# A selective-scan kernel on Trainium2: scan tiles of 64 pairs by 16 steps, increments written as pairs of steps, transposes between the first product's blocks

## The chip, the cores and the metric

The program runs on one core of one Trainium2 chip. The metric is the device time of one execution in microseconds (us). A core has TensorE (matmul; the profile shows its weight loads apart, as PEld), VectorE (DVE), ScalarE (ACT), GpSimd (POOL), SyncE (SP, which here only issues DMAs), and 16 DMA engines.

## The reference

Input x is 4 sequences of 2048 tokens with 256 channels. After a layer norm comes a Mamba block (512 inner channels, state 64), then a residual, a second layer norm and a gated FFN:

```
xn = layernorm(x) * ln_w + ln_b
xi, z = split(xn @ W_in)                     # 512 + 512
u = silu(causal_conv4(xi) + conv_b)
dt_r, B, C = split(u @ W_xproj)              # 16, 64, 64
delta = softplus(dt_r @ W_dt + b_dt)
A = -exp(A_log)                              # 512 x 64
for t in range(2048):                        # h: 4 x 512 x 64
    h = h * exp(delta[t] * A) + (delta[t] * u[t]) * B[t]
    y[t] = sum over the state of h * C[t]
block = x0 + ((y + u * D) * silu(z)) @ W_out # x0: the block's input
```

With `block` taken of layernorm(x), the output is:

```
x = x + block(layernorm(x))
x = x + w_down @ (silu(w_gate @ n) * (w_up @ n))   # n = layernorm(x), int weights / 127
```

## The kernel before, in words

Four stages follow each other: `norm_stage`, `project_stage`, `scan_stage`, `output_stage`. Every engine has its own list of instructions, written out by hand in loops; semaphores alone tie them together, so the order on an engine is the order in the code.

**project_stage** makes 16 steps, each over 512 tokens (tile i). TensorE: `front` (16 products `p_in`, L467), `back` (the rows of W_xproj and W_dt, L476 and L482), `turn` (60 transposes of 128x128 bf16 in eight groups, L497). ScalarE copies `xi` (L530), `sz` (L535), `u` (L542), `v`, takes Abs, Exp and Ln, then copies the transposes (`take_turns`, L577, L583). VectorE makes `softplus` (`p_w` L623 is its first row), the convolution of tile i+2 (`front`, L607, L610) and `split`, which divides delta and delta*u into three bf16 parts each (L641 to L647); GpSimd makes delta*u (L681) and the third parts (L685, L687, L689). The transposed parts of delta*u, named `u_turn`, go to the DRAM scratch `u_rows` in eight copies of 512 KB a tile, since one product later multiplies eight combinations of parts of delta*u and B at once. In `step` of TensorE the order is front(i+1), back(i), turn(i), and turn(i) works on the parts of tile i-1.

**scan_stage** makes 256 chunks of 32 steps. A pair is a channel of the lower and one of the upper half: 256 pairs, 64 states each, so that 128 partitions hold both. A chunk has eight tiles of 32 pairs by 32 steps. For a tile, TensorE makes the logits delta*A (L827) into `a_bank`, ScalarE their exponentials (L876) into `decay`; TensorE makes the increments delta*u*B (L849) into `u_bank`; GpSimd multiplies the last column of the chunk before by the first decay (`carry`, L952), adds the chunk's first increment (`seed`, L957) and sets that decay to 0; ScalarE copies `seed` into the first column of `u_bank` (L891); VectorE scans the tile's 1024 elements in one instruction (L917). The product with C (`contract`, L812) goes over the chunk before, two steps of each of four groups at a time, after every second tile. An fp32 product issues twice. `u_bank` holds two tiles: the increments of tile n wait for scan n-2. `H` holds two chunks. SyncE loads a chunk's `x2` (the parts of delta*u) with eight DMAs (L785) once the increments of the chunk before last have been made, and for every second chunk `x1`, `C` and `w2` (the parts of B).

The increment product in the code:

```
dst = u_bank[:, k % 2, 16 * b:16 * b + 16, 8 * e:8 * e + 8]
nc.tensor.matmul(dst.rearrange("p q t -> p t q"), w2[:, g, 4 * s + e, :], x2[:, s, :, e, q:q + 16], ...)
```

`u_bank` has the step innermost and the columns of this product run over the pairs first, so one column lies 32 words of fp32 behind the other.

## Time and profile before

| what | us |
|---|---|
| median of 3 runs (lowest, highest) | 6454.2 (6447.85, 6456.38) |
| the profiled execution's own time | 6459.31 |
| its span in the trace | 6457.5 |
| TensorE busy | 5991.9 (93%) |
| VectorE busy | 5512.5 (85%) |
| ScalarE busy | 3333.9 (52%) |
| GpSimd busy | 2099.4 (33%) |
| DMA moved | 452.03 MB |

How to read it: the shares of busy time are means over four stages. In the trace the transposes of the projection run until 957.85, the scans from 1021.24 to 5775, and the output stage's first DMA is issued at 5786.64; so each stage has to be read by itself. A matmul's end is modelled and matmuls overlap, so TensorE's busy share is not its load.

### The profile page before, as it was taken

The page shows a single profiled execution, that of the slowest core. Times are in us where ns is not written, and L with a number is a line of the kernel's source. Part 1 is how long each engine was busy: PE and PEld are TensorE (multiplying, and loading weights), DVE is VectorE, ACT ScalarE, POOL GpSimd, SP SyncE. Part 2 cuts the span into 40 slices and gives each one's busy share as a digit, 9 for nine tenths or more (in the row PEclk, how much of TensorE's full clock was granted, in tenths as well). Part 3 has the DMA queues.
Part 4 walks back from the last instruction along what each step waited for, and adds up shares of the span by engine and source line. Part 5 has one row for each costly group of instructions (what it writes and reads, how often), then busy time and mean ns, then how long its engine had stood idle before and what let it go on. Part 6 is the DMA issues. An engine that isn't in the chain of part 4 may idle for free. (4 is left out here: it accounts for less than half of the span.)

```text
span 6457.5 us, 156329 instructions
## 1 busy us (share of the span) xinstructions
PE 5991.9 (93%) x46272; PEld 3514.8 (54%) x46304; DVE 5512.5 (85%) x3489; ACT 3333.9 (52%) x7459; POOL 2099.4 (33%) x6848
## 2 busy tenths in 40 slices
PE   2787757999999999999999999999999999988999
PEld 1333324555555555555555555555555555546666
DVE  8566667999999999999999999999999999974443
ACT  1556654555555555555555555555555555541111
POOL 4233334333333333333333333333333333320000
PEclk9887778999999999999999999999999999999999
DMA  4476772111111111111111111111111111123331
GB/s 148 166 239 226 246 258 51 38 37 34 38 36 35 38 36 35 37 36 35 37 36 36 38 35 36 38 35 37 38 34 38 37 34 38 36 58 120 104 104 62
DMA packets 1133185, 452.03 MB, mean 70 GB/s; under 512 B 762608, under 2 KB 1088944, under 8 KB 1132736
## 3 DMA queue, kind: packets, MB, share of 16 engines
q1 hardware_dynamic: 1121456, 438.77, 25.6%
q10 hardware_dynamic: 11664, 12.52, 0.6%
q8 instruction: 26, 0.43, 0.0%
q14 instruction: 39, 0.32, 0.0%
HBM read 229.72 MB, written 221.77 MB: 70 GB/s over the span
## 5 line engine op out<-in xcount | busy, mean ns | idle before, releaser
L917 DVE TENSOR_TENSOR_SCAN s_h<-s_decay,s_ubank 128x1024 f32<-128x1024 f32 x2048 | 4572.2, 2274 | 206.6 <-ACT s_ubank L891 138.0
L876 ACT ACTIVATE s_decay<-s_abank 128x512 f32<-128x512 f32 x4096 | 2223.3, 596 | 1443.3 <-PE s_abank L827 1438.9
L849 PE MATMUL s_ubank<-s_x,s_w 128*128 128x128 bf16 x16384 | 2123.7, 309 | 0.1
L812 PE MATMUL s_ybank<-s_h,s_window 128*16 128x256 f32 x16448 | 1953.7, 603 | 1.8 <-DVE s_h L917 1.8
L849 PEld LDWEIGHTS s_ubank<-s_x,s_w 128*128 128x128 bf16 x16384 | 1715.7, 129 | 73.8 <-DVE s_h L917 0.4
L827 PE MATMUL s_abank<-s_x,s_a 128*128 128x256 bf16 x8192 | 1340.3, 280 | 55.5 <-DMA s_w<-scratch_b_rows 55.5
L952 POOL TENSOR_TENSOR s_carry<-s_decay,s_h 128x32 f32<-128x32 f32 x2016 | 592.2, 294 | 2297.6 <-ACT s_decay L876 2252.4
L827 PEld LDWEIGHTS s_abank<-s_x,s_a 128*128 128x128 bf16 x8192 | 708.2, 108 | 902.9 <-issue 709.0
L812 PEld LDWEIGHTS s_ybank<-s_h,s_window 128*16 128x16 f32 x16448 | 408.5, 104 | 820.0 <-issue 817.3
L957 POOL TENSOR_TENSOR s_seed<-s_carry,s_first 128x32 f32<-128x32 f32 x2048 | 518.2, 253 | 699.6 <-ACT s_first L885 559.2
L959 POOL TENSOR_TENSOR s_decay<-s_none 128x32 f32<-128x32 f32 x2048 | 510.0, 249 | 0.3
L891 ACT ACTIVATE s_ubank<-s_seed 128x32 f32<-128x32 f32 x2048 | 415.2, 203 | 136.8 <-PE s_ubank L849 2.4
L885 ACT ACTIVATE s_first<-s_firstbank 128x256 f32<-128x256 f32 x256 | 98.6, 385 | 450.6 <-PE s_firstbank L838 450.6
L1131 PE MATMUL o_gu<-o_xparts,o_wgu 128*128 128x512 bf16 x1120 | 250.9, 379 | 24.0 <-DVE o_hid L1234 22.2
L1175 ACT ACTIVATE o_sg<-o_gu 128x512 f32<-128x512 f32 x96 | 57.4, 598 | 410.1 <-PE o_gu L1131 409.3
L497 PE MATMUL p_turn<-p_ident,p_uparts 128*128 128x128 bf16 x816 | 96.9, 308 | 159.6 <-POOL p_b_parts L689 74.2
L467 PE MATMUL p_in<-xnT,p_w_in 128*128 (+1 forms) x512 | 228.1, 602 | 15.7 <-DMA p_b_dt<-in_b_dt 12.8
L1131 PEld LDWEIGHTS o_gu<-o_xparts,o_wgu 128*128 128x128 bf16 x1152 | 111.0, 98 | 159.2 <-DVE o_hid L1234 33.0
L497 PEld LDWEIGHTS p_turn<-p_ident,p_uparts 128*128 128x128 bf16 x816 | 79.0, 141 | 197.8 <-issue 119.6
L1141 PE MATMUL o_ob<-o_wd,o_hid 128*128 128x256 f32 x768 | 170.0, 381 | 10.6 <-DVE o_hid L1234 10.6
L467 PEld LDWEIGHTS p_in<-xnT,p_w_in 128*128 128x128 f32 x512 | 97.1, 193 | 136.0 <-issue 111.4
L476 PE MATMUL p_bk<-p_u,p_w_x 128*128 128x512 f32 (+1 forms) x384 | 170.7, 597 | 0.0
(121 smaller groups left out, 3019.2 us busy)
## 6 DMA issues: line engine op xcount, KB each, us to landing
scratch_u_rows<-p_u_turn SPq DMA_DIRECT2D x136, 512.0 KB, 5.7
scratch_delta_rows<-p_dparts SPq DMA_DIRECT2D x128, 512.0 KB, 5.7
s_x<-scratch_delta_rows SPq DMA_DIRECT2D x1024, 64.0 KB, 3.5
s_x<-scratch_u_rows SPq DMA_DIRECT2D x2048, 32.0 KB, 1.7
scratch_y<-s_y SPq DMA_DIRECT2D x1036, 16.0 KB, 1.4
scratch_sz<-p_sz SPq DMA_DIRECT2D x16, 1024.0 KB, 6.7
scratch_u<-p_u SPq DMA_DIRECT2D x16, 1024.0 KB, 8.2
s_w<-scratch_b_rows SPq DMA_DIRECT2D x256, 64.0 KB, 2.4
```

Source lines behind the costliest of these rows:

```text
L467: last = nc.tensor.matmul(in_bank[:, m % 2, :], w_in[:, k, m * P:(m + 1) * P], xnT[:, k, bass.ds(i * TW, TW)], start=(k == 0), stop=(k == ...
L497: last = nc.tensor.transpose(turn_bank[:, g % 2, n * P:(n + 1) * P], src, ident[:, :])
L812: last = nc.tensor.matmul(y_bank[32 * ct:32 * ct + WIN, 0:PAIRS], window[:, s, t * WIN:(t + 1) * WIN], H[s][:, :, t], start=(tt == 0), sto ...
L827: last = nc.tensor.matmul(a_bank[:, b, jj], a_w[:, half, j, :], x1[:, g, :, half, j, s * T:(s + 1) * T], start=True, stop=True)
L849: last = nc.tensor.matmul(dst.rearrange("p q t -> p t q"), w2[:, g, 4 * s + e, :], x2[:, s, :, e, q:q + 16], start=True, stop=True)
L876: nc.scalar.activation(decay[:, k % RING, 16 * b:16 * b + 16, :], a_bank[:, b].rearrange("p j r t -> p (j r) t"), ACT.Exp).then_inc(exp_do ...
L891: nc.scalar.activation(u_bank[:, k % 2, :, 0], seed[:, k % CPS, :], ACT.Identity).then_inc(seeded, 1)
L917: nc.vector.tensor_tensor_scan(H[s][:, PT * k:PT * k + PT, :].rearrange("p q t -> p (q t)"), decay[:, k % RING].rearrange("p q t -> p (q t)"),
L952: nc.gpsimd.tensor_tensor(carry[:, k % CPS, :], decay[:, k % RING, :, 0], before, ALU.mult).then_inc(carried, 1)
L957: nc.gpsimd.tensor_tensor(seed[:, k % CPS, :], carry[:, k % CPS, :], first[:, s, PT * k:PT * k + PT], ALU.add).then_inc(carried, 1)
L959: nc.gpsimd.tensor_tensor(decay[:, k % RING, :, 0], none[:, :], none[:, :], ALU.mult).then_inc(carried, 1)
L1131: last = nc.tensor.matmul(gu[:, m % 2, r, :], wgu[:, r, kk, m * P:(m + 1) * P], xparts[:, part, kk, :], start=(n == 0), stop=(n == 3 * KD ...
```

## The change

In the projection stage the eight groups of transposes are no longer behind `back`; one group stands behind each two products of `front`, on TensorE and on ScalarE, and turn(i) works on the parts of tile i-2. `back` makes the delta products before the rows of B and C, and ScalarE copies `b_in` and `c_out` after Ln. `du_rest` is gone (`du` is overwritten by its rest). `u_turn` becomes fp32: a bf16 part copied into it is the upper half of a word whose lower half is 0. Five copies of 1 MB go to `u_rows` in place of eight of 512 KB. In the diff `...` stands for what is left out.

In the scan stage a tile is 64 pairs by 16 steps (the same 1024 elements); tiles 0 to 3 of a chunk are its first 16 steps, 4 to 7 its last. Even rows r of an 8-step group are read from `u_rows` one bf16 element further on, so that a row of `x2` holds (value, 0) for an even step and (0, value) for an odd one, and one product with 256 columns writes pairs of neighbouring steps. Its loads are sixteen DMAs of 8 partitions. Logits and exponentials run five groups ahead (`LEAD`), `H` holds one chunk, and the first increments are made per half chunk (`firsts`), those of the next chunk's first half at tile 4.

```diff
-PT = 32
-TILES = PAIRS // PT
+TH = T // 2
+PT = 64
+BLOCKS = PAIRS // PT
+TILES = 2 * BLOCKS
+GROUPS = 8
+LEAD = 5
 GP = 2
-COMBOS = [(i, j) for j in range(3) for i in range(3) if i + j < 4]
+PARTS, PLACES = 3, 5
+COMBOS = [(i, j) for i in range(PARTS) for j in range(PARTS) if i + j < 4]
...
-WSTEPS = 8
+COPIES = (2, 2, 1, 1)
+WSTEPS = 4
...
-CONTRACT = {1: (0, 1), 3: (2, 3), 5: (4, 5), 7: (6, 7)}
+CONTRACT = {1: (0, 1), 3: (2, 3)}
...
+        u_turn = sb("p_u_turn", [P, PARTS, SUB, DI])
...
+            def turn_stores(i, last_one=False):
 
                 rows = bass.ds(i * TW, TW)
+                for part in range(3):
+                    sp.wait_ge(turn_read, i * 11 + 13 + 2 * part)
+                    for k, (_, j) in enumerate(COMBOS):
+                        if j == part and k < PLACES:
+                            sp.dma_start(d["u_rows"][rows, k, :].rearrange("(s p) q -> p s q", p=P),
+                                         u_turn[:, j, :, :].bitcast(BF16)).then_inc(turns_stored[j], 16)
...
             def step(i, c, b, ahead1, ahead2):
+                turn_stores(i)
                 if ahead1:
                     front_stores(*ahead1)
-                turn_stores(i)
                 back_stores(i, c, b)
...
             def step(i, c, b, ahead1, ahead2):
-                if ahead1:
-                    front(*ahead1)
+                for m in range(8):
+                    if ahead1:
+                        front(ahead1[0], m)
+                    turn(i, m)
                 back(i, c, b)
...
+                for m in range(8):
+                    if ahead1:
+                        front(ahead1[0], m)
+                    take_turn(i, m)
                 if ahead1:
-                    front(*ahead1)
+                    middle(*ahead1)
                 act.wait_ge(back_ready, i * 7 + 1)
...
+                        (du, du, uparts, (turned, i * 8 + 16), du_done, i + 3, u1_done, ur_done, u2_done)):
...
-                dve.wait_ge(turned, i * 8 + 8)
-                dve.wait_ge(b3_done, i + 1)
+                dve.wait_ge(back_read, i * 7 + 13)
+                dve.wait_ge(turned, i * 8 + 16)
+                dve.wait_ge(b3_done, i + 2)
...
+                pool.wait_ge(u3_done, i + 2)
...
-        H = [sb(f"s_h{s}", [P, PAIRS, T]) for s in range(2)]
-        decay = sb("s_decay", [P, RING, PT, T])
+        H = sb("s_h", [P, 2, PAIRS, TH])
+        decay = sb("s_decay", [P, 3, BLOCKS, PT, TH])
...
+        x2 = sb("s_x2", [P, 2, 4, 4, PAIRS, 2], BF16)
...
+            def widened(r, lo, f):
+
+                src = us[r, 2 * lo:2 * lo + 8, bass.ds(f * 4 + 2 * TW // 8, 4), :]
+                return src if r % 2 else bass.AP(src.tensor, src.offset + 1, src.ap)
...
+                    for lo in range(2):
+                        at = 16 * r + 8 * lo
+                        sp.dma_start(x2[at:at + 8, c % 2, r // 2].rearrange("p e q t -> p e (q t)"),
+                                     widened(r, lo, f)).then_inc(u_loaded[c % 2], 16)
...
+                of, at = (s, 0) if x else (1 - s, TH)
                 for tt in parts:
                     for ct in range(4):
                         t = ct * WSTEPS + tt
...
+            def firsts(it, f, c, x):
+
+                g, s = c // 2, c % 2
+                if x == 0:
+                    pe.wait_ge(u_loaded[s], it * 512 + g * 256 + 256)
+                pe.wait_ge(first_read, f * 2 + x + 1)
+                nc.tensor.matmul(first_bank[:, :, :], w2[:, g, 4 * s + 2 * x, :], x2[:, s, 0, 2 * x],
+                                 start=True, stop=True).then_inc(first_ready, 1)
...
                 s, g = c % 2, c // 2
                 for k in range(TILES):
-                    n = f * TILES + k
+                    n, x, p = f * TILES + k, k // BLOCKS, k % BLOCKS
                     if k == 0:
-                        pe.wait_ge(u_loaded[s], it * 256 + (c // 2) * 128 + 128)
-                        pe.wait_ge(first_read, f + 1)
-                        nc.tensor.matmul(first_bank[:, 0:PAIRS], w2[:, g, 4 * s, :], x2[:, s, 0, 0, :],
-                                         start=True, stop=True).then_inc(first_ready, 1)
-                    if k < TILES - 1:
-                        logits(it, n + 1, c, k + 1)
+                        firsts(it, f, c, 1)
+                    if k == 4 and not last_one:
+                        firsts(it + (c + 1) // 4, f + 1, (c + 1) % 4, 0)
+                    if k + LEAD < GROUPS:
+                        logits(it, f, c, k + LEAD)
                     elif not last_one:
-                        logits(it + (c + 1) // 4, n + 1, (c + 1) % 4, 0)
-                    pe.wait_ge(scan_done, n + 3)
+                        logits(it + (c + 1) // 4, f + 1, (c + 1) % 4, k + LEAD - GROUPS)
+                    pe.wait_ge(scan_done, n + 7)
                     for b in range(2):
-                        q = PT * k + 16 * b
-                        for e in range(4):
-                            dst = u_bank[:, k % 2, 16 * b:16 * b + 16, 8 * e:8 * e + 8]
-                            last = nc.tensor.matmul(dst.rearrange("p q t -> p t q"), w2[:, g, 4 * s + e, :],
-                                                    x2[:, s, :, e, q:q + 16], start=True, stop=True)
+                        q = PT * p + 32 * b
+                        for e in range(2):
+                            dst = u_bank[:, k % 2, 32 * b:32 * b + 32, 8 * e:8 * e + 8]
+                            last = nc.tensor.matmul(dst.rearrange("p q (a t) -> p a q t", t=2), w2[:, g, 4 * s + 2 * x + e, :],
+                                                    x2[:, s, :, 2 * x + e, q:q + 32, :], start=True, stop=True)
                     last.then_inc(u_ready, 1)
-                    if k in CONTRACT:
-                        contract(f, 1 - s, CONTRACT[k])
-
-            logits(0, 0, 0, 0)
+                    if p in CONTRACT:
+                        contract(f, s, x, CONTRACT[p])
...
+            def exps(f, c, kk):
+
+                n, p, at = f * GROUPS + kk, kk // 2, 32 * (kk % 2)
+                step = 1 + c % 2
+                act.wait_ge(scan_done, f * TILES + 1 + p)
                 for b in range(2):
                     act.wait_ge(a_ready, n * 2 + b + 65)
-                    nc.scalar.activation(decay[:, k % RING, 16 * b:16 * b + 16, :],
-                                         a_bank[:, b].rearrange("p j r t -> p (j r) t"),
+                    dst = decay[:, 0:step + 1:step, p, at + 16 * b:at + 16 * b + 16, :]
+                    nc.scalar.activation(dst.rearrange("p x q t -> p q x t"),
+                                         a_bank[:, b].rearrange("p j r (x t) -> p (j r) x t", x=2),
                                          ACT.Exp).then_inc(exp_done, 1)
...
-                    n = f * TILES + k
-                    if k == 0:
-                        dve.wait_ge(y_ready, f + 1)
+                    n, x, p = f * TILES + k, k // BLOCKS, k % BLOCKS
+                    if p == 0:
+                        dve.wait_ge(y_ready, f * 2 + x + 1)
                     dve.wait_ge(carried, n * 3 + 3)
                     dve.wait_ge(seeded, n + 1)
                     nc.vector.tensor_tensor_scan(
-                        H[s][:, PT * k:PT * k + PT, :].rearrange("p q t -> p (q t)"),
-                        decay[:, k % RING].rearrange("p q t -> p (q t)"),
+                        H[:, x, PT * p:PT * p + PT, :].rearrange("p q t -> p (q t)"),
+                        decay[:, x * (1 + c % 2), p].rearrange("p q t -> p (q t)"),
                         u_bank[:, k % 2].rearrange("p q t -> p (q t)"), 0.0,
...
-                    pool.wait_ge(exp_done, n * 2 + 4)
...
+                    n, x, p = f * TILES + k, k // BLOCKS, k % BLOCKS
+                    before = none[:, :] if fresh and x == 0 else H[:, 1 - x, PT * p:PT * p + PT, TH - 1]
+                    decays = decay[:, x * (1 + s), p, :, 0]
+                    pool.wait_ge(exp_done, f * 16 + 4 * p + 6)
...
+    scratch("u_rows", [TOK + 2 * TW, PLACES, 2 * DI], BF16)
```

TensorE's queue in the projection, one step, from its last products on. Before (`p_in` is `front`, `p_bk` is `back`, `p_turn` is `turn`):

```order
L481 REGISTER_ALU
L482 MATMUL p_bk<-p_dtr,p_w_dt 128x512 x2
L481 REGISTER_ALU
L482 MATMUL p_bk<-p_dtr,p_w_dt 128x512
L481 REGISTER_ALU
L482 MATMUL p_bk<-p_dtr,p_w_dt 128x512
L490 ISA
L497 MATMUL p_turn<-p_ident,p_uparts 128x128 x8
L490 REGISTER_ALU
L497 MATMUL p_turn<-p_ident,p_uparts 128x128 x8
L490 REGISTER_ALU
L497 MATMUL p_turn<-p_ident,p_uparts 128x128 x8
```

Now, the end of the first products of a step:

```order
L478 MATMUL p_in<-xnT,p_w_in 128x512 x2
L505 REGISTER_ALU
L512 MATMUL p_turn<-p_ident,p_b_parts 128x128 x8
L476 REGISTER_ALU
L478 MATMUL p_in<-xnT,p_w_in 128x512 x2
L505 REGISTER_ALU
L512 MATMUL p_turn<-p_ident,p_b_parts 128x128 x4
L489 ISA
L490 ISA
L485 MATMUL p_bk<-p_u,p_w_x 16x512 x4
L494 REGISTER_ALU
L495 MATMUL p_bk<-p_dtr,p_w_dt 128x512 x2
```

The transposes have moved from behind the delta products in between the `p_in` products, and the delta products (`p_dtr`) follow the 16-row ones at once.

TensorE's queue in the scan, two tiles and the product with C. Before:

```order
L849 MATMUL s_ubank<-s_x,s_w 128x8x16 x8
L824 ISA
L827 MATMUL s_abank<-s_x,s_a 128x256 x2
L824 REGISTER_ALU
L827 MATMUL s_abank<-s_x,s_a 128x256 x2
L844 REGISTER_ALU
L849 MATMUL s_ubank<-s_x,s_w 128x8x16 x8
L807 ISA
L808 REGISTER_ALU
L812 MATMUL s_ybank<-s_h,s_window 16x256 x8
L824 ISA
L827 MATMUL s_abank<-s_x,s_a 128x256 x2
```

Now, from the increments of tile 3 to those of tile 4:

```order
L891 MATMUL s_ubank<-s_x,s_w 128x4x32x2 x4
L846 MATMUL s_ybank<-s_h,s_window 8x256 x8
L869 ISA
L870 ISA
L871 MATMUL s_firstbank<-s_x,s_w 128x512
L858 ISA
L861 MATMUL s_abank<-s_x,s_a 128x256 x2
L858 REGISTER_ALU
L861 MATMUL s_abank<-s_x,s_a 128x256 x2
L886 REGISTER_ALU
L891 MATMUL s_ubank<-s_x,s_w 128x4x32x2 x4
```

The increments of a tile are four issues in place of eight, and the `first` product of the next chunk (its wait for the loads is L869) stands at tile 4, ahead of that tile's logits and increments.

## Rows read from the trace of the kernel before

**Rows 1.** Page: costliest groups, busy us, mean ns | idle before, releaser

```profile
L917 DVE TENSOR_TENSOR_SCAN s_h<-s_decay,s_ubank 128x1024 f32<-128x1024 f32 x2048 | 4572.2, 2274 | 206.6 <-ACT s_ubank L891 138.0
L876 ACT ACTIVATE s_decay<-s_abank 128x512 f32<-128x512 f32 x4096 | 2223.3, 596 | 1443.3 <-PE s_abank L827 1438.9
```

**Rows 2.** VectorE in order of time, 3008 to 3045: start us, us, what

```profile
3008.19 4.47 DVE L917 TENSOR_TENSOR_SCAN s_h<-s_decay,s_ubank 128x1024 f32<-128x1024 f32 x2 [0.24 <-ACT s_ubank L891]
3012.85 13.67 DVE L917 TENSOR_TENSOR_SCAN s_h<-s_decay,s_ubank 128x1024 f32<-128x1024 f32 x6 [0.19 <-ACT s_ubank L891]
3026.76 4.46 DVE L917 TENSOR_TENSOR_SCAN s_h<-s_decay,s_ubank 128x1024 f32<-128x1024 f32 x2 [0.24 <-ACT s_ubank L891]
```

**Rows 3.** All engines in order of time, 3000 to 3020, same columns

```profile
3003.44 1.04 PE L849 MATMUL s_ubank<-s_x,s_w 128*128 128x128 bf16 x8
...
3009.18 1.90 PE L812 MATMUL s_ybank<-s_h,s_window 128*16 128x256 f32 x16
...
3011.01 0.61 PE L827 MATMUL s_abank<-s_x,s_a 128*128 128x256 bf16 x4
...
3011.46 1.04 PE L849 MATMUL s_ubank<-s_x,s_w 128*128 128x128 bf16 x8
...
3012.61 0.20 ACT L891 ACTIVATE s_ubank<-s_seed 128x32 f32<-128x32 f32 x1
```

**Rows 4.** Matmuls of three lines, ns min/median/max; one in time; windows with PEclk

```profile
L849 PE MATMUL s_ubank<-s_x,s_w x688: 272/314/314, 3002.1 to 3199.2; 128*128 128x128 bf16 x172
...
L827 PE MATMUL s_abank<-s_x,s_a x344: 272/273/314, 3001.6 to 3198.4; 128*128 128x256 bf16 x172
...
L497 PE MATMUL p_turn<-p_ident,p_b_parts x12: 219/219/230, 925.6 to 926.7; 128*128 128x128 bf16 x12
...
924.67 0.62 PE L497 MATMUL p_turn<-p_ident,p_uparts 128*128 128x128 bf16 x8 [0.29 <-ACT p_u_turn L577]
...
3004.00:3041.00 37.00, 37.00 (x324) 21.76 (x322) 35.58 (x17) 21.10 (x53) 12.93 (x53) 1.00 0.18 36
...
923.00:925.00 2.00, 1.16 (x18) 0.82 (x16) 1.97 (x2) 2.00 (x3) 0.00 (x0) 1.00 1.04 354
```

**Rows 5.** SyncE's queue in order of time, 3004 to 3045; last row: us to landing

```profile
3004.69 1.41 SPq L782 DMA_DIRECT2D s_w<-scratch_b_rows  x2
3006.31 4.08 SPq L785 DMA_DIRECT2D s_x<-scratch_u_rows  x8
3010.65 1.91 SPq L767 DMA_DIRECT2D scratch_y<-s_y  x4
...
3029.69 5.92 SPq L777 DMA_DIRECT2D s_x<-scratch_delta_rows  x8
...
s_x<-scratch_u_rows SPq DMA_DIRECT2D x2048, 32.0 KB, 1.7
```

**Rows 6.** All engines in order of time, 500 to 620 (one projection step)

```profile
503.38 1.23 DVE L623 TENSOR_SCALAR p_w<-p_ex 128x2048 f32<-128x2048 f32 x1 [6.59 <-ACT p_ex L566]
...
529.73 0.43 DVE L657 CAST p_b_parts<-p_b_in 128x512 bf16<-128x512 f32 x1
...
544.26 4.18 POOL L687 TENSOR_TENSOR p_uparts<-p_du_rest,p_uparts 128x2048 bf16<-128x2048 f32 x1 [3.49 <-DVE p_uparts L647]
...
548.41 1.15 POOL L689 TENSOR_TENSOR p_b_parts<-p_b_rest,p_b_parts 128x512 bf16<-128x512 f32 x1
...
551.11 1.23 DVE L623 TENSOR_SCALAR p_w<-p_ex 128x2048 f32<-128x2048 f32 x1 [6.59 <-ACT p_ex L566]
...
554.21 1.92 ACT L577 ACTIVATE p_u_turn<-p_turn 128x1024 bf16<-128x1024 bf16 x2
...
555.27 1.95 PE L497 MATMUL p_turn<-p_ident,p_uparts 128*128 128x128 bf16 x16 [3.59 <-ACT p_u_turn L577]
...
561.08 14.23 PE L467 MATMUL p_in<-xnT,p_w_in 128*128 x32
```

**Rows 7.** Stretch of one projection step: busy us per engine, PEclk, DMA share, GB/s

```profile
515.00:563.00 48.00, 37.58 (x126) 17.32 (x125) 32.96 (x29) 29.23 (x38) 17.13 (x6) 0.79 0.69 235
```

More of the change, by code:

```diff
@@ L379, in project_stage @@
         sz_stored = sem("sz_stored")
-        c_stored = [sem("c_stored0"), sem("c_stored1")]
+        c_stored = sem("c_stored")
         dparts_stored = sem("dparts_stored")
-        turns_stored = sem("turns_stored")
+        turns_stored = [sem(f"turns_stored{j}") for j in range(4)]
         n_weights = 10
@@ L452, in _ @@
+            turn_stores(NT + 1, True)
             for s in range(2):
                 sp.wait_ge(u_stored[s], 16 * (NT // 2 + 1))
[L454 removed]
             sp.wait_ge(sz_stored, 16 * (NT + 1))
             sp.wait_ge(dparts_stored, 16 * NCB * (NT + 1))
[L457 removed]
+            sp.wait_ge(c_stored, 16 * (NT + 1))
+            for j in range(4):
+                sp.wait_ge(turns_stored[j], 16 * COPIES[j] * (NT + 3))
@@ L461, in _, with front, rows @@
             pe.wait_ge(weights, 16 * n_weights)
[L463 to L469 removed]
+            def front(i, m):
+                pe.wait_ge(in_read, i * 8 + m + 1)
+                for k in range(KD):
+                    last = nc.tensor.matmul(in_bank[:, m % 2, :], w_in[:, k, m * P:(m + 1) * P],
+                                            xnT[:, k, bass.ds(i * TW, TW)], start=(k == 0), stop=(k == KD - 1))
+                last.then_inc(in_ready, 1)
             def back(i, c, b):
[L472 to L474 removed]
+                def rows(bank, lo, n):
                     for m in range(MI):
@@ new lines, in back, with turn @@
+                rows(0, RANK, 2 * NS)
+                rows(1, RANK + 2 * NS, 2 * NS)
+            def turn(i, g):
+                if g == 0:
+                    pe.wait_ge(u3_done, i + 1)
+                    pe.wait_ge(b3_done, i + 1)
+                pe.wait_ge(turn_read, i * 11 + (9, 11, 12, 13, 14, 15, 16, 17)[g])
+                for n in range(8 if g < 7 else 4):
+                    if g < 6:
+                        at = (2 * (g % 2) + n // 4) * P
+                        src = uparts[:, g // 2, n % 4, at:at + P]
+                    else:
+                        src = b_parts[:, 2 * (g - 6) + n // 4, n % 4 * P:(n % 4 + 1) * P]
+                    last = nc.tensor.transpose(turn_bank[:, g % 2, n * P:(n + 1) * P], src, ident[:, :])
+                last.then_inc(turned, 1)
@@ L816, in contract, with logits @@
                     last.then_inc(y_ready, 1)
-            def logits(it, n, c, k):
-                g, s, half, j0 = c // 2, c % 2, k // 4, 4 * (k % 4)
-                if k == 0 and s == 0:
+            def logits(it, f, c, kk):
+                g, s, half, j0, n = c // 2, c % 2, kk // 4, 4 * (kk % 4), f * GROUPS + kk
+                if kk == 0 and s == 0:
                     pe.wait_ge(rows_loaded[g], it * 176 + 176)
@@ L856, in _ @@
+                    last.then_inc(u_ready, 1)
+                    if p in CONTRACT:
+                        contract(f, s, x, CONTRACT[p])
+            for kk in range(LEAD):
+                logits(0, 0, 0, kk)
+            firsts(0, 0, 0, 0)
             over_chunks_peeled(pe, chunk)
-            contract(NF, 1, tuple(range(WSTEPS)))
+            contract(NF, NF % 2, 0, tuple(range(WSTEPS)))
         @block.scalar
```

256 lines of the change are left out of this document (115 added, 141 removed).

## The prediction

> **What bounds the kernel now.** I read the costliest groups first, then VectorE's rows in order of time, then all engines around one chunk of the scan, then SyncE's queue, then one step of the projection stage, and last the stretches with their clock and DMA share.
>
> The groups [rows 1] say that the time lies in the scan: 2048 scans of 2274 ns are 4657 us of the 6457.5 us span. VectorE's rows [rows 2] show one chunk: 3008.19 to 3026.76 is 18.57 us for eight scans. Six in a row take 13.67 us, so 2.278 us each; eight would take 18.22. What is left is 0.35 us a chunk, in two gaps released by ScalarE's seed copy; over 256 chunks 89 us, the most that the scan stage can give back while its scans stay as they are. (The group's 206.6 us of idle time is too much: 4572.2 / 2.274 is 2011 scans, so 37 of the 2048 are missing from the records and count as idle.)
>
> Why the gap: TensorE [rows 3]. It runs the `y` product from 3009.18 to 3011.08, logits from 3011.01, increments from 3011.46, and ScalarE's seed at 3012.61 follows the increments' end at 3012.50; the scan starts at 3012.85, late. Two tiles of TensorE's work take 4.60 us, VectorE's two scans 4.56: two near-equal bounds. One increment product, 128 columns, takes 314 ns where a transpose of 128 columns at the same granted clock (1.00, so 2.4 GHz) takes 219, and eight come at a spacing of (1.04 - 0.314) / 7 = 0.104 us, as wide as the spacing of logits with 256 columns, (0.61 - 0.273) / 3 = 0.112 [rows 3, 4]. So these write at half the pace of the others; what sets them apart is an output that jumps 128 bytes from column to column.
>
> The projection stage takes 47.7 us a step (503.38 to 551.11) for 16 steps, and no engine is full: in one step TensorE is busy 37.6 of 48, VectorE 33, DMA 0.69 [rows 6, 7]. It is bounded by a chain: the transposes stand behind the last product and before the next step's first one (561.08), and ScalarE copies them between Ln and `xi` (554.21 on).
>
> **The change, part by part.**
>
> *Scan: increments.* 64 products of 128 columns a chunk become 32 of 256, whose inner run is two adjacent steps (8 bytes). Bounds for one: 0.107 us (the pace of the logits) and 0.21 (two of today's). I take 0.107, because the row shows the pace halved for single words and the pair keeps the 8 bytes together. A tile's increments then take 0.43 us instead of 0.86, two tiles save 0.86, and TensorE's 4.60 falls to about 3.75, well under 4.56. VectorE's gap goes: -89 us.
>
> *Scan: the rest of the tile.* The scan stays 128x1024, and products of `y` stay at 16 issues every second tile. Exponentials keep their 512 elements, now in runs of 16, and I take today's 596 ns [rows 1]; nothing in the rows has such runs. Walking one pair from the end of a scan at 0: increments 0.1 to 0.7, `y` product to 2.3, logits' first half at 2.7, two exponentials to 3.9, seed to 4.2; the scan it feeds is due at 4.56. So 0.3 us cover a dearer exponential; beyond that each excess costs four times a chunk. GpSimd's three operations a tile grow from 32 to 64 elements; it is busy 12.93 of 37.00 us [rows 4], and twice that still fits. `take_y` and `firsts` come twice a chunk: 0.8 us of ScalarE more in 18.2, behind the seed; hidden.
>
> *Scan: loads of the increments' operand.* This is where a wait is added. Eight loads a chunk become sixteen on SyncE's queue, and the first product that needs them moves from tile 0 to tile 4 of the chunk before. Today eight loads take 4.08 us from 3006.31, 0.51 each, and land 1.7 us after issue [rows 5]; in even chunks two loads of `w2` come first, so they begin 1.83 us after the increments that free the buffer ended (3004.48) [rows 3, 5]. Bounds for a new one: 0.48 (a store of `y`, 16 packets, 1.91 us for four) and 0.74 (a load of `x1`, 512 packets, 5.92 us for eight). It has 32 packets of 1 KB instead of 64 of 512 B, so I take 0.51. The last lands at 1.83 + 15 x 0.51 + 1.7 = 11.2 after the buffer is free, which is 11.9 after the scan end that I count from. TensorE reaches tile 4 at four scans (9.1) + 0.1 + 0.4 + 1.8 = 11.4. Behind it wait logits, increments, exponentials and the seed: 11.9 + 0.1 + 0.2 + 0.4 + 1.1 + 0.4 = 14.1; the scan is due at six scans, 13.67. So even chunks lose 0.45 us, odd ones (no `w2`, 1.6 earlier) nothing: 128 x 0.45 = +58 us. SyncE's issue time for two chunks is about 1.4 + 2 x 4.1 + 2 x 1.9 + 5.9 = 19.3 us and rises to 27.5 of 36.4, so it is no bound by itself.
>
> *Scan: ends.* The first chunk waits for eight more loads: +4. The last `y` product is half as long (32 issues of 0.107 less): -3.
>
> *Projection.* Transposes of tile i-2 now stand between the products of tile i+1, ScalarE takes them between `xi` and `sz`, and the delta products come before those of B and C. The old chain breaks up. What is late next: the single copy of `uparts`. From the first transposes to the last are 7 products of 14.23 / 8 = 1.78 us and 7.5 groups of eight at half of (1.95 - 0.25), 0.85: 18.8 us. Then VectorE splits, 529.73 to 544.26, 14.5 us; GpSimd takes the last parts, 4.2 + 1.15; hand-overs 0.5. Sum 39.2 us, and I take 39.3 [rows 6]. Bounds: 36.2 us from the DMAs, and 47.7 (nothing gained). For the DMAs: 235 GB/s at a share of 0.69 is 341 at full; a step moves 11.3 MB and five stores of 1 MB instead of eight of 0.5 add 1.05: 12.3 / 0.341 = 36.2 [rows 7]. Fifteen intervals, the last without a product: 14 x 8.4 + 2 = -120 us. The second extra round of transposes is in the old tail already, since the last tile's were waited for there too: 0.
>
> **Sum.** -120 - 89 + 58 + 4 - 3 = -150. The profiled execution took 6459.3 us, so 6309; the median of the runs shown is 5 us lower, so **6304**.
>
> **A rule against the trace.** The half pace of the scattered writes is this trace's own [rows 4]. The Trainium skill, "PSUM — Partial Sum Buffer", section "Specifications (TRN2)", gives 8-byte cachelines and adds that any non-contiguous pattern slows matmuls significantly. The first half fits pairs at full pace; the second half, read strictly, leaves them slow, which is the first rival.
>
> **Rivals.**
> 1. *Pairs write no faster per column.* For it: the output still jumps 64 bytes after every pair. Against: nothing in the rows has pairs. TensorE keeps 4.60 us for two tiles and gets two `first` products of 512 columns where it had one of 256, at the logits' 0.112 per 256 columns 0.34 us more: 18.57 + 0.34 = 18.91 a chunk, +87 us. With -120 and +1: **6422**. By the strict reading of that page this would be the outcome.
> 2. *Everything in time.* The sixteen loads land before tile 4, and TensorE, with fewer pauses, keeps the upper clock in the transposes (a group of eight took 0.62 us at clock 1.00, against half of 1.95 [rows 4, 6]), so that the step falls to the DMAs' 36.5: 14 x 11.2 + 2 = -159, -89, +1: **6207**.
> 3. *The loads decide (slower).* Place: the wait for `u_loaded` before `firsts` at tile 4. If a load takes 0.65 us instead of 0.51 (half-way to `x1`'s), even chunks lose 0.45 + 15 x 0.14 = 2.55 us and odd ones 0.93, 3.48 a pair: 128 x 3.48 - 89 = +356, and with -120 **6691**. It turns the sign from 1.6 us a pair, a load of 0.59. For it: the new loads reach 8 partitions, and half of them start 2 bytes off. Against: issue time hardly depends on packets (0.48 with 16, 0.51 with 64).
> 4. *The projection gains little*, because stores of 0.94 DMA share hold back buffers or VectorE and GpSimd slow each other: 45 us a step, -40, -31: **6383**.
>
> **Chances.** The forecast 0.55, rival 1 0.13, rival 2 0.15, rival 3 0.10, rival 4 0.07. A measurement of this kernel tells 0.2% (13 us) from no change. Rival 3 is slower by more than that, with 0.01 for others: 0.11; 0.04 within it (the upper end of rival 1, a mild form of 3); 0.85 faster. The range runs from rival 2 to the upper side of rival 1, 6205 to 6440, and leaves out rival 3 and half of rival 2's lower side.
>
> **What would show it.** Increments of 256 columns at a median near 273 ns and a group of four in about 0.6 us (rival 1: 480 and 0.9); scans back to back, a chunk of 18.2 us odd and 18.7 even, the gap in front of tile 4 with a DMA as TensorE's releaser; the interval between two `p_w` on VectorE at 39 us, with VectorE waiting for transposes before the cast of `b_parts`; DMA share there above 0.9; the output stage unchanged. I am wrong if the scans themselves lengthen, if the gaps move to another tile with ScalarE's exponentials as releaser, or if the step stays over 43 us.

## The result and the profile after

| what | before, us | after, us |
|---|---|---|
| median (lowest, highest), 4 runs each | 6455.29 (6447.85, 6457.26) | 6155.88 (6154.45, 6157.07) |
| span of the profiled execution | 6457.5 | 6152.6 |
| up to the first scan | 1021.2 | 928.4 |
| first scan to the end of the last | 4753.8 | 4547.5 |
| behind the last scan | 682.5 | 676.7 |

The ratio is 0.954, 95% interval 0.952 to 0.956. The forecast of 6304 us had the sign, and 148 us too little gain; its range ended at 6205. Of 304.9 us of span, 92.8 were gained up to the first scan, 206.3 in the scan stage (forecast: 31) and 5.8 behind it.

The page of the changed kernel, costliest groups (busy us, mean ns | idle before, releaser):

```profile
L971 DVE TENSOR_TENSOR_SCAN s_h<-s_decay,s_ubank 128x1024 f32<-128x1024 f32 x2048 | 4499.2, 2267 | 81.6 <-ACT s_ubank L940 80.4
L923 ACT ACTIVATE s_decay<-s_abank 128x512 f32<-128x512 f32 x4096 | 2234.9, 604 | 1763.5 <-PE s_abank L861 1763.5
...
L861 PE MATMUL s_abank<-s_x,s_a 128*128 128x256 bf16 x8192 | 1425.4, 276 | 310.9 <-DMA s_x<-scratch_u_rows 73.6
```

A scan's record is hardly shorter than before (2267 ns against 2274, [rows 1]), and the exponentials in their runs of 16 take 604 ns against 596. VectorE in order of time (start us, us, what, [idle before <- releaser]):

```profile
2989.65 26.37 DVE L971 TENSOR_TENSOR_SCAN s_h<-s_decay,s_ubank 128x1024 f32<-128x1024 f32 x12
3016.34 35.15 DVE L971 TENSOR_TENSOR_SCAN s_h<-s_decay,s_ubank 128x1024 f32<-128x1024 f32 x16 [0.32 <-ACT s_ubank L940]
3051.92 35.15 DVE L971 TENSOR_TENSOR_SCAN s_h<-s_decay,s_ubank 128x1024 f32<-128x1024 f32 x16 [0.42 <-ACT s_ubank L940]
```

Sixteen scans take 35.15 us, 2.197 each, where [rows 2] gave 2.278: less than the 2.26 us that a record lasts, so neighbouring records overlap. Two chunks take 3051.92 - 3016.34 = 35.58 us against 2 x 18.57. One gap is left in two chunks; TensorE's queue in order of time shows what it waits for, and SyncE's what came late:

```profile
3011.73 0.61 PE L891 MATMUL s_ubank<-s_x,s_w 128*128 128x256 bf16 x4
3012.27 1.90 PE L846 MATMUL s_ybank<-s_h,s_window 128*8 128x256 f32 x16
3014.68 0.60 PE L861 MATMUL s_abank<-s_x,s_a 128*128 128x256 bf16 x4 [0.52 <-DMA s_x<-scratch_u_rows]
```

```profile
3003.79 1.43 SPq L813 DMA_DIRECT2D s_w<-scratch_b_rows  x2
3005.52 7.24 SPq L818 DMA_DIRECT2D s_x<-scratch_u_rows  x16
3013.03 1.71 SPq L799 DMA_DIRECT2D scratch_y<-s_y  x4
```

Four increment products of 256 columns take 0.61 us where eight of 128 took 1.04 [rows 3]: pairs write at full pace, as forecast. TensorE's wait stands at tile 4 with a DMA behind it, as forecast, and VectorE's gap is 0.32 to 0.42 us against 0.45. The sixteen loads take 7.24 us, 0.45 each (0.51 taken).

One projection step, VectorE, GpSimd and the last transposes of TensorE in order of time:

```profile
496.85 4.18 POOL L713 TENSOR_TENSOR p_uparts<-p_du,p_uparts 128x2048 bf16<-128x2048 f32 x1 [3.49 <-DVE p_uparts L672]
497.02 5.09 DVE L650 TENSOR_SCALAR p_w<-p_ex 128x2048 f32<-128x2048 f32 x1
500.99 2.13 POOL L715 TENSOR_TENSOR p_b_parts<-p_b_rest,p_b_parts 128x512 bf16<-128x512 f32 x1
502.14 3.13 DVE L652 SCALAR_TENSOR_TENSOR p_ex<-p_w,p_ex 128x2048 f32<-128x2048 f32 x1
...
509.84 5.94 DVE L634 TENSOR_SCALAR p_acc<-p_xi,p_conv_w 128x512 f32<-128x512 f32 x4
510.06 4.63 POOL L707 TENSOR_TENSOR p_du<-p_lw,p_u 128x2048 f32<-128x2048 f32 x1 [6.94 <-DVE p_lw L658]
...
520.59 0.39 PE L512 MATMUL p_turn<-p_ident,p_b_parts 128*128 128x128 bf16 x4
...
524.02 0.43 DVE L682 CAST p_b_parts<-p_b_in 128x512 bf16<-128x512 f32 x1
...
530.08 4.99 POOL L711 TENSOR_TENSOR p_dparts<-p_w,p_dparts 128x2048 bf16<-128x2048 f32 x1 [3.49 <-DVE p_dparts L672]
531.17 6.04 DVE L670 TENSOR_TENSOR p_du<-p_du,p_uparts 128x2048 f32<-128x2048 f32 x1
538.73 5.08 DVE L650 TENSOR_SCALAR p_w<-p_ex 128x2048 f32<-128x2048 f32 x1
```

The step is 538.73 - 497.02 = 41.7 us, against 47.7 before and 39.3 forecast. The addition `p_w` took 1.23 us [rows 6] and takes 5.09 beside GpSimd's 4.18: it ends 1.1 us after GpSimd has ended. Two signs that the forecast named are absent: VectorE doesn't wait for transposes ahead of the cast of `b_parts` (the last of them ended 3.0 us earlier), and the DMA share is 0.83 and not above 0.9. A window over five steps (busy us of PE, PEld, DVE, ACT, POOL; PEclk, DMA share, GB/s) has VectorE busy nearly all the time, 198 of 200 us:

```profile
450.00:650.00 200.00, 178.40 (x609) 77.98 (x608) 198.18 (x142) 138.59 (x175) 84.73 (x25) 0.87 0.83 294
```

### The profile page after: what moved, and what is told of

The parts are those of the page before. It is cut to its first block and busy times, and to the rows that moved or that the text cites. A ratio compares the mean times of both kernels' runs of the same rounds, so it can differ in the third digit from the quotient of the medians.

```text
span 6152.6 us, 147986 instructions
## 1 busy us (share of the span) xinstructions
PE 5492.5 (89%) x37915; PEld 2419.3 (39%) x38396; DVE 5559.3 (90%) x3491; ACT 3328.5 (54%) x7982; POOL 2612.2 (42%) x6848
## 5 line engine op out<-in xcount | busy, mean ns | idle before, releaser
L971 DVE TENSOR_TENSOR_SCAN s_h<-s_decay,s_ubank 128x1024 f32<-128x1024 f32 x2048 | 4499.2, 2267 | 81.6 <-ACT s_ubank L940 80.4
L846 PE MATMUL s_ybank<-s_h,s_window 128*8 128x256 f32 x16416 | 1948.2, 602 | 1.9 <-DVE s_h L971 1.9
L1008 POOL TENSOR_TENSOR s_carry<-s_decay,s_h 128x64 f32<-128x64 f32 x2032 | 882.3, 434 | 1781.3 <-ACT s_decay L923 1030.3
L891 PE MATMUL s_ubank<-s_x,s_w 128*128 128x256 bf16 x8192 | 1234.7, 273 | 38.3 <-DVE s_h L971 4.0
L891 PEld LDWEIGHTS s_ubank<-s_x,s_w 128*128 128x128 bf16 x8192 | 735.9, 98 | 288.3 <-DVE s_h L971 183.0
L1012 POOL TENSOR_TENSOR s_seed<-s_carry,s_first 128x64 f32<-128x64 f32 x2048 | 657.9, 321 | 164.4 <-ACT s_first L929 4.0
L846 PEld LDWEIGHTS s_ybank<-s_h,s_window 128*8 128x8 f32 x16416 | 377.2, 97 | 838.6 <-issue 835.5
L1014 POOL TENSOR_TENSOR s_decay<-s_none 128x64 f32<-128x64 f32 x2048 | 619.9, 303 | 0.0
L940 ACT ACTIVATE s_ubank<-s_seed 128x64 f32<-128x64 f32 x2048 | 495.8, 242 | 72.6 <-PE s_ubank L891 9.1
L996 POOL TENSOR_TENSOR s_window<-s_c,s_none 64x32 f32<-64x32 f32 x512 | 130.7, 255 | 406.8 <-PE s_ybank L846 386.6
L913 ACT ACTIVATE s_y<-s_ybank 128x256 f32<-128x256 f32 x514 | 198.4, 386 | 6.8 <-PE s_ybank L846 6.8
```

The costliest lines, as they stand in the source:

```text
L846: last = nc.tensor.matmul(y_bank[32 * ct:32 * ct + WIN, 1 - x, :], window[:, of, (at + t) * WIN:(at + t + 1) * WIN], H[:, 1 - x, :, t], st ...
L891: last = nc.tensor.matmul(dst.rearrange("p q (a t) -> p a q t", t=2), w2[:, g, 4 * s + 2 * x + e, :], x2[:, s, :, 2 * x + e, q:q + 32, :], ...
L940: nc.scalar.activation(u_bank[:, k % 2, :, 0], seed[:, k % CPS, :], ACT.Identity).then_inc(seeded, 1)
L971: nc.vector.tensor_tensor_scan(H[:, x, PT * p:PT * p + PT, :].rearrange("p q t -> p (q t)"), decay[:, x * (1 + c % 2), p].rearrange("p q t ...
L1008: nc.gpsimd.tensor_tensor(carry[:, k % CPS, :], decays, before, ALU.mult).then_inc(carried, 1)
L1012: nc.gpsimd.tensor_tensor(seed[:, k % CPS, :], carry[:, k % CPS, :], first[:, x, PT * p:PT * p + PT], ALU.add).then_inc(carried, 1)
```

## The experiments

Two questions: why the scan stage gained 206 us where 89 was held to be the most, and why the step stopped at 41.7 us.

**1. The kernel before, increments written flat.**

```diff
-dst = u_bank[:, k % 2, 16 * b:16 * b + 16, 8 * e:8 * e + 8]
+bank = u_bank[:, k % 2, 16 * b:16 * b + 16, :].rearrange("p q t -> p (q t)")
+dst = bank[:, 128 * e:128 * e + 128].rearrange("p (t q) -> p t q", q=16)
...
```

> The kernel before, its increments written as 128 consecutive words a product instead of words 128 bytes apart. The words land in other places of the bank, so the kernel computes other states; amount and kind of work are those of before. Theory (TensorE set the scan stage, its scattered increments with it, and VectorE's own spacing is the 2.197 us of the changed kernel): increments 314 -> about 220 ns, a group of eight about 0.6 us instead of 1.04, scans at 2.197 us, a chunk 17.6 us instead of 18.57, time 6455 - 256 x 0.97 = about 6207. Rival (2.278 us is the scan's own pace in the layout of 32 pairs by 32 steps, and the changed kernel is faster by its layout of 64 by 16): a chunk 18.22 us, time 6455 - 89 = about 6366. Rival (the pace of a product doesn't depend on where it writes): 314 ns and 6455 unchanged.

Measured: 6164.3 us, ratio 0.955 (0.953 to 0.957), with nothing else of the change in it. Increments take 219 ns. Those products (ns min/median/max):

```profile
L850 PE MATMUL s_ubank<-s_x,s_w x736: 218/219/231, 3000.9 to 3198.8; 128*128 128x128 bf16 x184
```

VectorE in order of time:

```profile
2997.90 52.36 DVE L918 TENSOR_TENSOR_SCAN s_h<-s_decay,s_ubank 128x1024 f32<-128x1024 f32 x24
```

24 scans of the old layout at 52.36 / 24 = 2.18 us. The layout of the changed kernel is not the cause; TensorE was, through its scattered writes. [rows 4] had it: TensorE was busy 37.00 of 37.00 us there, VectorE 35.58. The flat kernel gave 43 us more than my 6207, since even 2.197 was not the floor.

**2. The changed kernel, single words again.**

```diff
-matmul(dst.rearrange("p q (a t) -> p a q t", t=2), ..., x2[:, s, :, 2 * x + e, q:q + 32, :])
+matmul(dst.rearrange("p q (a t) -> p a t q", t=2), ..., x2[...].rearrange("p a q t -> p a t q"))
```

> The changed kernel, with the order in which an increment product writes turned round: the steps of a pair are no longer written one behind the other, so that each word lands 64 bytes from the one before. Same values in the same places. Theory (pairs are what made the products quick, and TensorE becomes the bound again without them): a product of 256 columns about 0.21 us instead of 0.107 in a row, two tiles of TensorE 4.6 us or more, a chunk 18.6 to 18.9 us instead of 17.8 on average, time 6156 + 256 x 1.0 = 6360 to 6450. Rival (the scans are quicker for another reason than TensorE, their new layout): scans stay at 2.197 us, time within 20 us of 6156.

Measured: 6422.4 us, 267 more than with pairs. The increment products (ns min/median/max, and four of them in order of time):

```profile
L891 PE MATMUL s_ubank<-s_x,s_w x342: 379/417/418, 3001.0 to 3200.0; 128*128 128x256 bf16 x171
...
3010.51 1.03 PE L891 MATMUL s_ubank<-s_x,s_w 128*128 128x256 bf16 x4
```

VectorE in order of time:

```profile
3007.33 9.05 DVE L971 TENSOR_TENSOR_SCAN s_h<-s_decay,s_ubank 128x1024 f32<-128x1024 f32 x4 [0.43 <-ACT s_ubank L940]
3016.72 9.05 DVE L971 TENSOR_TENSOR_SCAN s_h<-s_decay,s_ubank 128x1024 f32<-128x1024 f32 x4 [0.34 <-ACT s_ubank L940]
```

417 ns instead of 273, four in 1.03 us instead of 0.61, and four scans at 9.05 us, 2.26 each, without a shown gap: the slow spacing of [rows 2] comes back with TensorE's load. A chunk is 2 x 9.39 = 18.8 us. Experiments 1 and 2 settle it from both sides.

With that known, [rows 2] can be read again. Single scans of the kernel before (ns min/median/max, start of the first and the last):

```profile
L917 DVE TENSOR_TENSOR_SCAN s_h<-s_decay,s_ubank x2: 2262/2274/2287, 3010.4 to 3012.8; 128x1024 f32<-128x1024 f32 x2
...
L917 DVE TENSOR_TENSOR_SCAN s_h<-s_decay,s_ubank x2: 2262/2274/2287, 3012.8 to 3015.0; 128x1024 f32<-128x1024 f32 x2
...
L917 DVE TENSOR_TENSOR_SCAN s_h<-s_decay,s_ubank x2: 2262/2274/2287, 3015.0 to 3017.4; 128x1024 f32<-128x1024 f32 x2
```

The starts are 2.4, 2.2, 2.4 us apart. In the row "x6, 13.67 us" every second scan was late by about 0.2 us: 0.08 of it is hidden in the overlap of the records, and the rest was too short to break the row. A late scan reads 2287 ns, a prompt one 2262. Two scans are 4.6 us apart (3010.4 to 3015.0, 3012.8 to 3017.4), which is TensorE's 4.60 for two tiles.

**3. First products behind tile 6 instead of tile 4** (`if k == 4` becomes `if k == 6`, on TensorE and ScalarE).

> The changed kernel, with the first products of the next chunk's first half put behind tile 6 instead of tile 4. Theory (they wait there for the loads of delta*u in even chunks, and that wait is the 0.42 us gap of VectorE): the gap goes, a chunk is 8 x 2.197 = 17.58 us in both kinds, time 6156 - 128 x 0.42 = about 6102, and TensorE shows no wait for a DMA. Rival (the 0.9 us of first products, now a tile closer to the increments that need them, makes another scan late): the gap moves to tile 7 or 0 of the next chunk and the time is 6156 or above.

Measured: 6090.8 us, 65 less, the whole of it between first and last scan (4547.5 to 4482.6). TensorE's list of waits has no DMA left, and VectorE runs without a break:

```profile
2999.01 52.60 DVE L971 TENSOR_TENSOR_SCAN s_h<-s_decay,s_ubank 128x1024 f32<-128x1024 f32 x24
```

So the late loads cost 65 / 128 = 0.51 us per even chunk. The gap of 0.42 us showed this too small, by the 0.08 us that two records overlap otherwise.

**4. GpSimd's third part of delta*u nearly left out.**

```diff
-nc.gpsimd.tensor_tensor(uparts[:, 2], du[:, :, :], uparts[:, 1], ALU.subtract)
+nc.gpsimd.tensor_tensor(uparts[:, 2, :, 0:16], du[:, :, 0:16], uparts[:, 1, :, 0:16], ALU.subtract)
```

> The changed kernel; of the third bf16 part of delta*u GpSimd makes only 16 of 512 columns, the rest stays zero, so GpSimd's 4.17 us beside VectorE's p_w addition are nearly gone. Theory (GpSimd's operation holds VectorE's up, and VectorE is the bound of the projection step): p_w takes 1.23 us as alone, instead of 5.09, the step falls from 41.7 to 37.9 us, time 6156 - 15 x 3.8 = about 6099. Rival (p_w is slow because of the DMA traffic or its operands): p_w stays at 5.09 and the time near 6156. Rival (VectorE isn't the bound): p_w 1.23, VectorE waits instead, step and time unchanged.

Measured: 6099.7 us and a step of 37.95, as the theory had it:

```profile
512.13 1.33 DVE L650 TENSOR_SCALAR p_w<-p_ex 128x2048 f32<-128x2048 f32 x1
...
550.08 1.33 DVE L650 TENSOR_SCALAR p_w<-p_ex 128x2048 f32<-128x2048 f32 x1
```

GpSimd's operation causes the 5.09 us, and VectorE is the bound: what it no longer loses, the step gains in full.

**5. `p_w` on ScalarE** (activation Identity with a bias of 1.0, in place of VectorE's addition).

> The changed kernel, with the addition p_w = ex + 1 made by ScalarE (1.9 us, behind its exponential) instead of VectorE. Theory (VectorE bounds the step of 41.70 us; what GpSimd's 4.17 us of work holds up is whichever VectorE operation stands beside it, so the subtraction that now stands there is held up in place of p_w): only the addition's own 1.23 us go, step about 40.5, time 6156 - 15 x 1.2 = about 6138. Rival (only the cheap one-operand additions are held up): all 5.09 us go from VectorE and the chain of my forecast takes over at 39.2 us, time 6156 - 15 x 2.5 = about 6118, with VectorE idle. Rival (VectorE isn't the bound): 6156 or, if ScalarE's 1.9 us stand in the chain, up to 6185.

Measured: 6141.0 us, 15 less, as the theory had it (6138). The hold-up has passed to the operation behind (2.29 us when alone):

```profile
532.22 4.19 POOL L717 TENSOR_TENSOR p_uparts<-p_du,p_uparts 128x2048 bf16<-128x2048 f32 x1 [3.49 <-DVE p_uparts L676]
...
532.89 5.67 DVE L656 SCALAR_TENSOR_TENSOR p_ex<-p_w,p_ex 128x2048 f32<-128x2048 f32 x1 [0.41 <-ACT p_w L587]
```

**6. Transposes behind all first products again.**

```diff
                 for m in range(8):
                     if ahead1:
                         front(ahead1[0], m)
+                for m in range(8):
                     turn(i, m)
```

(ScalarE's copies likewise.)

> The changed kernel, with the eight groups of transposes and their copies all behind the eight first products again, and everything else left (sizes, VectorE's and GpSimd's order, delta products first). Theory (VectorE is the bound at 41.7 us, interleaving hides work that was hidden by then): step within 1 us of 41.70, time 6150 to 6170. Rival (the interleaving is what brought the step down from 47.7): step 45 to 48 us, time 6156 + 15 x 3.3 to 6.3 = 6205 to 6250, VectorE idle before p_w with ScalarE's exponential as releaser.

**7. The products of B and C first again**, with ScalarE's copies of them; interleaving kept.

> The changed kernel with the products of B and C ahead of the delta products again (and ScalarE's copies with them); interleaved transposes stay. Theory (VectorE bounds the step; this order gives slack that isn't used): 41.7 us as before, 6150 to 6165, maybe a wait of 1 us at p_w. Rival (the early delta products are what brought 47.7 down): they come about 8 x 0.7 = 5.7 us later, step 44 to 47.7, time 6190 to 6245.

**8. Both moves undone.**

> The changed kernel with both moves undone: transposes behind all first products and products of B and C first. What is left of the change in this stage is that tile i-2 is transposed instead of i-1, the same for the stores, and the double time that the split parts may stay. Theory (each move alone gives enough slack, both together are needed to undo it): p_w waits again for ScalarE's exponential, step 44 to 47.7, time 6190 to 6245. Rival (the lag of two tiles alone is what took the transposes out of the chain): 42 to 43 us, time 6155 to 6180.

Measured: 6166.3 us (6), 6160.9 (7), 6259.9 (8). Either move alone brings nearly all, since 10 and 5 us are what its absence costs; without both, 104 are lost, the step is 47.7 us on average (772.63 - 247.84 over 11), and the old wait is back, in VectorE's row of the last kernel:

```profile
514.50 1.23 DVE L652 TENSOR_SCALAR p_w<-p_ex 128x2048 f32<-128x2048 f32 x1 [9.88 <-ACT p_ex L589]
```

What (8) leaves of the change in this stage (the lag of two tiles, the fp32 `u_turn`, the five copies of 1 MB) gives nothing by itself.

The expectation for (7), that VectorE bounds the step and has slack, held for the time and not for the mechanism. VectorE's row there:

```profile
548.02 1.42 DVE L650 TENSOR_SCALAR p_w<-p_ex 128x2048 f32<-128x2048 f32 x1 [3.59 <-ACT p_ex L587]
```

VectorE waits 3.6 us for ScalarE, GpSimd's 4.18 us pass meanwhile, and `p_w` takes 1.42 us instead of 5.09: the wait stands where the hold-up stood, and the step stays at 41.7. That the early delta products would be worth more in a kernel without the hold-up follows from this row; no run shows it.

**9. Three edits: experiments 3 and 5, and the first tap of the convolution on ScalarE.**

> The changed kernel with three edits together: first products behind tile 6, p_w on ScalarE, and the first tap of the convolution (four products with a constant, 5.94 us a step beside GpSimd) on ScalarE too. Scan stage as with the first edit alone: -65. Projection, theory (VectorE is the bound, GpSimd's two long operations of 4.17 and 4.63 us then hold up the operations behind): of 41.70 go 1.23 and four times 0.35 us, 41.70 - 2.6 = 39.1, time 6156 - 65 - 15 x 2.6 = about 6052. Rival (the operations that come beside GpSimd now are not held up): 5.1 + 5.9 us go and the chain of my forecast binds at 39.2 or ScalarE's work (30.5 + 4.3 us busy, with its table loads) does: 6050 to 6060 as well, but with VectorE idle 8 us a step and its operations at the length that they have alone. Rival (ScalarE becomes the bound): step above 41.7, time above 6091.

Measured: 6059.2 us, with a step of 39.35 us on average. The time lies near the theory's 6052 and within the first rival's 6050 to 6060, so the rows have to tell them apart. GpSimd, TensorE and VectorE in order of time:

```profile
523.12 4.20 POOL L721 TENSOR_TENSOR p_uparts<-p_du,p_uparts 128x2048 bf16<-128x2048 f32 x1 [3.49 <-DVE p_uparts L680]
527.28 3.20 POOL L723 TENSOR_TENSOR p_b_parts<-p_b_rest,p_b_parts 128x512 bf16<-128x512 f32 x1
530.72 0.62 PE L515 MATMUL p_turn<-p_ident,p_uparts 128*128 128x128 bf16 x8 [1.94 <-POOL p_b_parts L723]
...
534.87 12.30 DVE L648 SCALAR_TENSOR_TENSOR p_acc<-p_xi,p_conv_w,p_acc 128x512 f32<-128x512 f32 x12
...
535.10 4.90 POOL L715 TENSOR_TENSOR p_du<-p_lw,p_u 128x2048 f32<-128x2048 f32 x1 [4.62 <-DVE p_lw L666]
...
547.94 0.39 PE L515 MATMUL p_turn<-p_ident,p_b_parts 128*128 128x128 bf16 x4
548.37 0.43 DVE L690 CAST p_b_parts<-p_b_in 128x512 bf16<-128x512 f32 x1 [0.99 <-PE p_turn L515]
```

The twelve taps take 12.30 us where the changed kernel has 8.03: held up again, by 4.3, which speaks against that rival. But VectorE is no longer the bound either (busy 185 of 200 us). In every second step it waits for the transposes ahead of the cast of `b_parts`, which starts 0.04 us after the last of them has ended: the chain of the forecast binds there, with 39.8 us from cast to cast (508.60 to 548.37). It was a true bound, but not the first one. Its total came out by two errors that nearly cancel: the split takes 14.5 us as forecast, GpSimd's last parts 7.4 where 5.35 were taken (`p_b_parts` takes 3.20, not 1.15), and the transposes 17.6 where 18.8 were taken.

**10. All five GpSimd operations of the step on VectorE**, on top of experiment 3.

```diff
+dve.wait_ge(two, i + 1)
+nc.vector.tensor_tensor(parts[:, 2], rest[:, :, :], parts[:, 1], ALU.subtract).then_inc(three, 1)
...
+nc.vector.tensor_tensor(du[:, :, :], lw[:, :, :], u[:, c % 2], ALU.mult).then_inc(du_done, 1)
```

> The changed kernel with first products behind tile 6 (6091 us), and GpSimd's five operations of the projection step put on VectorE, each at the place where its result is due. Theory (beside each of GpSimd's operations VectorE stands still for nearly all its time, so GpSimd gives nothing and costs its slower pace): of VectorE's 41.7 us about 12.4 are held-up time (3.9 at p_w, 0.8 at p_ex, 4.0 at the first tap, 2.9 and 0.8 at the two subtractions); they go, and three operations of 2.3 and two of 0.6 us come: 41.7 - 12.4 + 8.1 = 37.4 us a step, time 6091 - 15 x 4.3 = about 6026. Rival (the two engines do overlap, the rows only share the delay out otherwise): VectorE gets 8.1 to 18 us more to do, a step of 45 or more, time above 6140.

**11. The same with experiment 9's two edits.**

> As the kernel before in this list, with p_w and the first tap on ScalarE as well. Theory: VectorE falls to 37.4 - 1.2 - 2.0 = 34.2 us and something else takes over: the DMAs (share 0.88 at a step of 39.8 us in the kernel with three edits, so 35 us at full) or ScalarE (34.3 us busy); a step of 35 to 36.5 us, VectorE with 1 to 3 us idle, time 6091 - 15 x 5.5 = about 6005 to 6015. Rival (VectorE still sets it, by the handovers to ScalarE in the softplus): 37 us or more, time 6020 or above.

Measured: 6018.2 us (10) and 6017.1 (11). VectorE's step in (10), in order of time:

```profile
502.36 2.29 DVE L674 TENSOR_TENSOR p_uparts<-p_du,p_uparts 128x2048 bf16<-128x2048 f32 x1
...
505.63 1.22 DVE L650 TENSOR_SCALAR p_w<-p_ex 128x2048 f32<-128x2048 f32 x1
...
542.30 1.22 DVE L650 TENSOR_SCALAR p_w<-p_ex 128x2048 f32<-128x2048 f32 x1
```

The window over five steps of it:

```profile
450.00:650.00 200.00, 189.47 (x651) 80.96 (x650) 195.53 (x184) 155.25 (x195) 0.00 (x0) 0.92 0.95 337
```

A step of 542.30 - 505.63 = 36.7 us with GpSimd idle (the theory had 37.4 us and 6026). VectorE needs 2.29 us for what took GpSimd 4.18 and cost VectorE 3.9 meanwhile. The held-up time, from 41.70 to 36.67 with 8.25 us of work added, is 13.3 of GpSimd's 18.0 us a step. In (11) VectorE is unloaded by 2.9 us more and nothing comes of it; its window shows what is full now, TensorE (190 of 200) and the DMAs (0.95):

```profile
450.00:650.00 200.00, 189.94 (x659) 81.15 (x658) 179.97 (x158) 177.45 (x226) 0.00 (x0) 0.92 0.95 335
```

The list of waits of this window names no DMA. TensorE's own pauses end with ScalarE: at `p_sz` 5.1 us in five waits, at `p_dtr` 4.1 in six. So the trace points to TensorE and its hand-overs with ScalarE and not to the DMAs; no run takes load off TensorE alone, so it isn't shown by an edit. The expectation for (11), 6005 to 6015 us from a step of 35 to 36.5, failed: unloading VectorE gained 1 us, which is no difference between these runs.

**12. First products at tiles 5 and 1 instead of 6 and 0**, on top of experiment 10.

> The kernel with GpSimd's projection work on VectorE (6018 us, first products at tiles 6 and 0), with the first products moved to tiles 5 and 1. At even tiles they stand behind the product with C, on TensorE's longest stretch, and the kernel before with flat increments runs its scans at 2.179 us, this one at 2.189; one scan in four or so is 2289 ns long instead of 2261. Theory (the scan behind such a first product is released late by 0.05 to 0.1 us, and no idle time shows): scans at 2.18 us, all near 2261 ns, 2048 x 0.010 = -20 us, time about 5998. Rival (GpSimd's wider operations hold the scans up, or the scan's pace depends on the layout): 6018 unchanged.

Measured: **5993.3 us**, ratio to the kernel before 0.9285 (0.927 to 0.930), the best of all. VectorE in order of time:

```profile
2999.34 61.06 DVE L966 TENSOR_TENSOR_SCAN s_h<-s_decay,s_ubank 128x1024 f32<-128x1024 f32 x28
```

All its scans in 200 us (ns min/median/max):

```profile
L966 DVE TENSOR_TENSOR_SCAN s_h<-s_decay,s_ubank x93: 2261/2261/2262, 2999.3 to 3199.7; 128x1024 f32<-128x1024 f32 x93
```

None of these 93 scans reads 2287 ns any more. The scan stage takes 4461.2 us, 2.178 a scan, the same as experiment 1's 4461.7 in the other layout: this is the pace of such scans when their operands lie ready, and the least that any run here needed.

## Why the prediction was wrong

*Increments.* Right: pairs at the pace of the logits, 0.107 us in a row taken, 0.60 to 0.61 us for four measured. Rival 1 is out, and so is the strict reading of the Trainium skill, "PSUM — Partial Sum Buffer", section "Specifications (TRN2)": a pattern that jumps 64 bytes after every 8 was not slowed. With single words (experiment 2) it was, to half the pace: four in 1.03 us.

*VectorE's gap, -89: the step that failed.* "Six in a row take 13.67 us, so 2.278 us each; eight would take 18.22. What is left is 0.35 us a chunk ... the most that the scan stage can give back." The division took six scans that TensorE released late for six at VectorE's own pace. The two bounds named as near-equal, 4.60 and 4.56 us for two tiles, were one: the second was the first seen through VectorE. VectorE's own was 2 x 2.178 = 4.36, so a chunk could shrink from 18.57 us to 17.42. With the loads in time (experiment 3) it came to 4482.6 / 256 = 17.51: 4753.8 to 4482.6, -271 instead of -89. The trace of the kernel before held the warning, and the forecast argued it away. It took 37 scans to be missing from the records, since 4572.2 us of busy time are only 2011 times 2.274. None is missing: all 2048 are there, and neighbouring records overlap by 0.08 us. So 4753.8 - 4572.2 = 181.6 us of idle time in the scan stage were real, twice the 89.

*Loads late, +58.* Right in place, kind and chunk; +65 measured by experiment 3. Rival 3 is out. The size is partly luck: the sixteen loads were issued in 7.24 us and not in 8.2, which makes the wait shorter, and the scans that TensorE follows came at 2.2 us and not at 2.278, which makes it longer.

*Start and ends, +4 and -3.* The output side came to -5.8. The start isn't seen apart from the projection.

*Projection, -120.* -93 up to the first scan. The chain of 39.2 us is real (experiment 9), but VectorE was costed by its busy time in the kernel before, 33 of 48 us, and the new order puts `p_w`, the operation behind it and the first taps beside GpSimd, which adds 3.9 + 0.8 + 4.0 us: 41.7. The kernel before had shown such a hold-up, in a subtraction that takes 2.29 us when GpSimd is idle (experiment 10):

```profile
535.79 4.98 POOL L685 TENSOR_TENSOR p_dparts<-p_w,p_dparts 128x2048 bf16<-128x2048 f32 x1 [3.49 <-DVE p_dparts L647]
536.88 6.04 DVE L645 TENSOR_TENSOR p_du_rest<-p_du,p_uparts 128x2048 f32<-128x2048 f32 x1
```

The forecast had this as half of rival 4, at 45 us and a chance of 0.07. The Trainium skill has the mechanism in "SBUF — State Buffer", section "SBUF: two separate sides": VectorE and GpSimd share a pair of ports under an exclusive lock, held for a whole instruction, and it concerns VectorE where it reads two inputs from SBUF or runs in a two-port mode. The trace agrees (5.09 us beside 4.18, 1.23 alone), and the scans, which read one input from PSUM, were not held (2261/2261/2262 ns with GpSimd at work). Whether `p_w`, which reads one input, runs in a two-port mode no run shows. The lock was not weighed in the forecast and should have been. The interleaving, which I took for the step that does it, is one of two moves of which either is enough at a step of 41.7 us.

*Sum by measured terms:* -93 - 271 + 65 - 6 = -305. Rival 2 (6207, everything in time) came nearest and for the wrong reasons: the loads were late, the step was not DMA-bound.
